# Many-head attention: tokens on the partitions in the product, one batch projected ahead of the other, values awaited later, norms by batch

## The reference

```
x = x + L2_attn(layernorm(x))    # 16 query heads of 16 wide, 4 key/value heads, causal
x = x + L2_ffn(layernorm(x))     # x @ (sum of 8 factor matrices) / sqrt(8) + bias
x = x + L3_xattn(layernorm(x))   # 16 heads of 128 wide over 2048 context tokens
x = x + L3_attn(layernorm(x))    # differential attention, see below
x = x + L3_ffn(layernorm(x))
# L2_attn
q, k, v = x @ Wq, x @ Wk, x @ Wv
out = softmax(causal(q k^T / 4)) v ;  return out @ Wo
# L3_attn: 32 half heads of 8 wide, values 16 wide, a pair of half heads per head
probs = softmax(causal(q k^T / sqrt(8)))
attn = (probs[0] - lam * probs[1]) v ; attn = attn * rms(attn) * g * 0.8 ; return attn @ Wo + bo
```

## Time and profile before

| | |
|---|---|
| timed runs (3) | median 1151.47 us, 1148.25 to 1151.93 |
| profiled execution | 1146.93 us |
| its span | 1145.0 us |
| PE busy | 1044.0 us, 91% of the span |
| DVE, ACT, POOL busy | 61%, 44%, 20% |
| mean granted clock of PE | 0.974 |

### The profile page before, as it was taken

One profiled execution on the slowest core, in us unless ns is written; L12 is line 12 of the kernel. 1 busy time (PEld: TensorE's weight loads), 2 busy tenths in 40 slices (PEclk: granted clock), 3 DMA queues, 4 the chain that ended last, 5 costly groups with the idle time before them and its releaser, 6 DMA issues.

```text
span 1145.0 us, 23185 instructions
## 1 busy us (share of the span) xinstructions
PE 1044.0 (91%) x9488; PEld 847.0 (74%) x9488; DVE 700.8 (61%) x1333; ACT 505.3 (44%) x871; POOL 233.2 (20%) x356
## 2 busy tenths in 40 slices
PE   6988999979999879999988799989999999999785
PEld 3755788856667546767765688889999999999664
DVE  3655343267776368888644666766656466667366
ACT  3232131226767248888764423332332222332374
POOL 5601058102132000000011311210001133332120
PEclk9999999989999889999999999999999999999897
DMA  9621447536652417000131211121111121100000
GB/s 389 266 77 76 148 168 224 174 92 173 177 161 80 162 49 244 2 2 2 41 145 37 92 37 38 36 103 47 38 39 55 46 76 56 56 20 10 0 2 10
DMA packets 39332, 104.57 MB, mean 91 GB/s; under 512 B 4160, under 2 KB 12736, under 8 KB 37568
## 3 DMA queue, kind: packets, MB, share of 16 engines
q1 hardware_dynamic: 35328, 91.55, 24.2%
q0 software_dynamic: 2752, 9.44, 2.4%
q10 hardware_dynamic: 1152, 2.16, 0.5%
HBM read 87.93 MB, written 15.20 MB: 90 GB/s over the span
## 4 chain that ended last, share of the span: by engine, by line
PE 74%; DVE 12%; ACT 5%; POOL 4%; issue 3%; DMA 2%; DVEq 0%; SPq 0%; ACTq 0%; POOLq 0%
PE ps L2184 9%; PE ps L390 8%; PE ps L2139 7%; PE ps L1372 5%; PE ps L1723 5%; PE ps L383 4%; PE ps L2029 4%; PE ps L446 3%; PE ps L1714 3%; PE ps L1520 3%; PE ps L2043 2%; PE ps L1058 2%; PE ps L1531 2%; PE ps L1050 2%; DVE st L1649 2%
## 5 line engine op out<-in xcount | busy, mean ns | idle before, releaser
L2184 PE MATMUL ps<-vv,prob 128*128 128x129 f32 x1024 | 128.7, 275 | 0.0
L2184 PEld LDWEIGHTS ps<-vv,prob 128*128 128x128 f32 x1024 | 122.5, 192 | 0.0
L2307 DVE TENSOR_REDUCE probT<-ps 128x128 f32<-128x1024 f32 x64 | 82.6, 1290 | 28.8 <-PE ps L2139 20.8
L1649 DVE TENSOR_REDUCE st<-ps 128x1 f32<-128x512 f32 x128 | 83.5, 687 | 25.3 <-PE ps L1520 19.1
L2074 ACT ACTIVATE kt<-ps,w 128x512 f32<-128x512 f32 x32 | 22.0, 688 | 141.8 <-PE ps L2051 141.8
L390 PE MATMUL ps<-xT,big 128*128 128x256 f32 x352 | 79.6, 380 | 0.8 <-ACT xT L673 0.7
L2319 DVE TENSOR_TENSOR prob<-ps,probT 128x1024 f32<-128x1024 f32 x64 | 79.6, 1286 | 1.1
L2280 ACT ACTIVATE prob<-prob 128x1024 f32<-128x1024 f32 x64 | 70.7, 1107 | 19.6 <-DVE prob L2319 19.6
L1596 ACT ACTIVATE prob<-ps 128x1024 f32<-128x1024 f32 x64 | 65.7, 1028 | 27.8 <-PE ps L1531 26.1
L152 POOL TENSOR_SCALAR small<-small 128x4 f32<-128x4 f32 (+1 forms) x44 | 12.0, 272 | 322.2 <-DVE small L2081 175.3
L390 PEld LDWEIGHTS ps<-xT,big 128*128 128x128 f32 x352 | 66.5, 190 | 10.7 <-ACT xT L673 0.9
(11 more groups left out here) (457 smaller groups left out, 2214.4 us busy)
## 6 DMA issues: line engine op xcount, KB each, us to landing
big<-ctxT_in SPq DMA_DIRECT2D x36, 512.0 KB, 4.1
big<-blocks_in SPq DMA_DIRECT2D x22, 768.0 KB, 4.4
key_parts<-w POOLq DMA_DIRECT2D x16, 384.0 KB, 4.7
kt<-key_parts SPq DMA_DIRECT2D x32, 192.0 KB, 3.3
vv<-ctx_in SPq DMA_DIRECT2D x2, 2176.0 KB, 23.9
vv<-early_values SPq DMA_DIRECT2D x4, 1088.0 KB, 12.9
kt<-ctxT_in SPq DMA_DIRECT2D x2, 2048.0 KB, 11.4
kt<-key_parts SPq DMA_DIRECT2D x32, 128.0 KB, 3.1
```

Source lines behind the costliest of these rows:

```text
L1649: dve.tensor_reduce(self.mx[:, u % 2, n:n + 1], k.ps[:, n % 2, :], AX.X, ALU.max).then_inc(s("reduced"), 1)
L2184: last = pe.matmul(k.ps[:, 7, 0:DH + 1], self.prob(u)[:, ch * P:ch * P + P], v, start=(ch == 0), stop=(ch == MC))
L2307: dve.tensor_reduce(self.largest[:, h * P:(h + 1) * P], bank.rearrange("p (c t) -> p t c", t=P), AX.X, ALU.max).then_inc(s("c3_max"), 1)
```

## The change

- `Heads.product`: `probT` (128x128) becomes the stationary operand and v with its ones (17 columns) the moving one. The result has tokens on the partitions, 17 columns per head, in bank 6 or 7 by turns. `ot`, `back` and the zeroing of bank 6 go; `finish` reads the product's bank; the reciprocals have two buffers.
- `Heads.tensor` takes two callbacks: `values_ready` waits ahead of product 0 for the values and the ones, which the layers awaited ahead of everything; `turn_first` turns batch 0 of `att` ahead of the last product.
- Both layers: v is projected into bank 6 instead of 2. Batch 0 is projected behind the last product, then batch 1 is turned, copied and projected. In L2 this replaces one turn, one copy and one projection of both batches; L3 did it by batch already, behind all units.
- Norms 7 to 10: each batch's transposes go to a bank of their own, each with a semaphore count, and ACT copies each batch; one count of `xT` at the end.
- Norm 10: the statistics of batch 0 are taken ahead of the wait for the last projection of batch 1.
- `Differential.vector`: the scaling of g is moved ahead of the wait for lam's exponentials.

```diff
+    BY_BATCH = {7: (7, 0), 8: (7, 2), 9: (7, 3), 10: (7, 3)}
...
+    def tensor_batches(k, pe, n):
+        for b, bank in enumerate(Norm.BY_BATCH[n]):
+            pe.wait_ge(k.s("norm_xn"), 2 * n + b + 1)
+            turn_batch(k, pe, k.xn, b, bank, 0).then_inc(k.s("norm_turned"), 1)
...
+    def scalar_batches(k, act, n):
+        for b, bank in enumerate(Norm.BY_BATCH[n]):
+            act.wait_ge(k.s("norm_turned"), Norm.turned_batches(n, b))
+            last = act.copy(k.xT[:, b].rearrange("p c t -> p (c t)"), k.ps[:, bank, 0:D])
+        last.then_inc(k.s("xT"), 1)
...
+def copy_att(k, act, b, count):
+    act.wait_ge(k.s("att_turned"), count)
+    act.copy(k.attT[:, b].rearrange("p c t -> p (c t)"), k.ps[:, b, 0:D]).then_inc(k.s("attT"), 1)
...
+    def output(self, i):
+        return self.k.ps[:, 6 + i % 2, 0:8 * 17].rearrange("p (h n) -> p h n", n=17)
...
-            if i >= 1:
-                pe.wait_ge(*self.at("ot", i))
+            if i >= 2:
+                pe.wait_ge(*self.at("out", i - 1))
             for h in range(8):
-                g = h % 4 * 32
-                last = pe.matmul(k.ps[g:g + 17, 6, h // 4 * P:h // 4 * P + P], self.v[:, b, kv(h)], k.probT[:, h * P:(h + 1) * P], start=True, stop=True)
+                last = pe.matmul(self.output(i)[:, h], k.probT[:, h * P:(h + 1) * P], self.v[:, b, kv(h)], start=True, stop=True)
             last.then_inc(self.s("product"), 1)
-        def back(i):
...
             if i + 2 < n:
                 scores(i + 2)
+            if i == 0:
+                values_ready()
+            if i == n - 1:
+                turn_first()
             product(i)
-            if i >= 1:
-                back(i - 1)
-        back(n - 1)
...
-        def ot(i):
...
-            dve.wait_ge(*self.at("back", i + 1))
+            dve.wait_ge(*self.at("product", i + 1))
...
-        o.step(dve.memset(k.ps[:, 6, 0:256], 0.0))
...
         pe.wait_ge(s("g2_sb"), 2)
-        pe.wait_ge(s("heads_ones"), 2)
-        self.heads.tensor(pe)
-        pe.wait_ge(s("att"), 2)
-        turn(k, pe, k.att, 7).then_inc(s("att_turned"), 1)
+        def values_ready():
+            pe.wait_ge(s("g2_sb"), 3)
+            pe.wait_ge(s("heads_ones"), 1)
+        def turn_first():
+            pe.wait_ge(s("heads_out"), 2)
+            turn_batch(k, pe, k.att, 0, 0, 0).then_inc(s("att_turned"), 1)
+        self.heads.tensor(pe, values_ready, turn_first)
         pe.wait_ge(s("attT"), 2)
-        for b in range(B):
-            last = project(k, pe, k.ps[:, 3, b * D:(b + 1) * D], k.attT, b, w("Wo", DC), D)
+        project(k, pe, k.ps[:, 3, 0:D], k.attT, 0, w("Wo", DC), D)
+        pe.wait_ge(s("heads_out"), 4)
+        turn_batch(k, pe, k.att, 1, 1, 0).then_inc(s("att_turned"), 1)
+        pe.wait_ge(s("attT"), 3)
+        project(k, pe, k.ps[:, 3, D:2 * D], k.attT, 1, w("Wo", DC), D).then_inc(s("out_projection"), 1)
...
-        act.copy(flat(self.heads.kk), k.bank(1))
+        act.copy(flat(self.heads.kk), k.bank(1)).then_inc(s("g2_sb"), 1)
...
+        dve.wait_ge(s("w_added"), 1)
+        Norm.stats(k, dve, o, 0)
         dve.wait_ge(s("w_wo"), 2)
-        dve.wait_ge(s("w_added"), 1)
         o.step(dve.tensor_tensor(k.x[:, 1], k.x[:, 1], k.ps[:, 6, 0:D], ALU.add))
+        Norm.stats(k, dve, o, 1)
...
         pe.wait_ge(s("e3_sb"), 3)
-        pe.wait_ge(s("e3_lam"), 2)
-        pe.wait_ge(s("heads_ones"), 4)
-        self.heads.tensor(pe)
+        def values_ready():
+            pe.wait_ge(s("e3_lam"), 2)
+            pe.wait_ge(s("heads_ones"), 2)
+        def turn_first():
+            pe.wait_ge(s("att"), 2)
+            turn_batch(k, pe, k.att, 0, 0, 0).then_inc(s("att_turned"), 1)
+        self.heads.tensor(pe, values_ready, turn_first)
...
         self.heads.scalar(act)
+        copy_att(k, act, 0, 4)
         self.table(act, ACT.Sqrt, 504)
-        self.copy_att(act, 0)
...
```

More of the change, by code:

```diff
@@ L216, in tensor, with turned_batches @@
         last.then_inc(k.s("norm_turned"), 1)
+    BY_BATCH = {7: (7, 0), 8: (7, 2), 9: (7, 3), 10: (7, 3)}
+    @staticmethod
+    def turned_batches(n, b):
+        return turned_norms(n - 1) + sum(i in Norm.BY_BATCH for i in range(n)) + b + 1
+    @staticmethod
+    def tensor_batches(k, pe, n):
+        for b, bank in enumerate(Norm.BY_BATCH[n]):
+            pe.wait_ge(k.s("norm_xn"), 2 * n + b + 1)
+            turn_batch(k, pe, k.xn, b, bank, 0).then_inc(k.s("norm_turned"), 1)
+    @staticmethod
+    def scalar_batches(k, act, n):
[3 more added lines that the diff above has]
+        last.then_inc(k.s("xT"), 1)
     @staticmethod
@@ L1288, in scalar @@
         act.wait_ge(s("g2_proj"), 2)
-        act.copy(flat(self.heads.kk), k.bank(1))
+        act.copy(flat(self.heads.kk), k.bank(1)).then_inc(s("g2_sb"), 1)
         act.wait_ge(s("g2_proj"), 3)
-        act.copy(self.heads.v[:, :, :, 0:16], k.bank(2, 128).rearrange("p (b h n) -> p b h n", b=B, h=4)).then_inc(s("g2_sb"), 1)
+        act.copy(self.heads.v[:, :, :, 0:16], k.bank(6, 128).rearrange("p (b h n) -> p b h n", b=B, h=4)).then_inc(s("g2_sb"), 1)
         self.heads.scalar(act)
-        act.wait_ge(s("att_turned"), 2)
-        act.copy(flat(k.attT), k.bank(7)).then_inc(s("attT"), 1)
+        copy_att(k, act, 0, 2)
+        copy_att(k, act, 1, 3)
     def vector(self, dve, o):
@@ L2499, in vector @@
         dve.sem_inc(s("e3_lam"), 1)
+        o.step(dve.tensor_scalar(self.g, w("g"), 0.8, None, ALU.mult))
         dve.wait_ge(s("e3_sb"), 1)
@@ L2765, in _ @@
             wide.value(pe, 5, 3)
-            Norm.tensor(k, pe, 7)
+            Norm.tensor_batches(k, pe, 7)
             pe.wait_ge(s("w_v_sb"), 4)
@@ L2769, in _ @@
             wide.value(pe, 2, 1)
-            Norm.tensor(k, pe, 8)
+            Norm.tensor_batches(k, pe, 8)
             pe.wait_ge(s("xT"), turned_norms(8))
@@ L2776, in _ @@
             wide.value(pe, 3, 2)
-            Norm.tensor(k, pe, 9)
+            Norm.tensor_batches(k, pe, 9)
             wide.tensor(pe)
-            Norm.tensor(k, pe, 10)
+            Norm.tensor_batches(k, pe, 10)
             differential.tensor(pe)
@@ L2827, in _ @@
             wide.copy_value(act, 5, 3)
-            Norm.scalar(k, act, 7)
+            Norm.scalar_batches(k, act, 7)
             Norm.table(k, act, ACT.Exp, 3)
@@ L2835, in _ @@
                 wide.copy_value(act, *((2, 1) if n == 8 else (3, 2)))
-                Norm.scalar(k, act, n)
+                Norm.scalar_batches(k, act, n)
             Norm.table(k, act, ACT.Exp, 5)
@@ L2841, in _ @@
                 Norm.root(k, act, 10, b)
-            Norm.scalar(k, act, 10)
+            Norm.scalar_batches(k, act, 10)
             differential.scalar(act)
@@ L2920, in _ @@
             wide.vector(dve, o, eight)
-            Norm.vector(k, dve, o, 10)
+            Norm.scaled(k, dve, o, 10)
             differential.vector(dve, o)
```

48 lines of the change are left out of this document (16 added, 32 removed).

## The result

The changed kernel takes 1159.56 us (median of 12 runs), the kernel before 1150.18 beside it: ratio 1.0087, 95% interval 1.0066 to 1.0108. One execution of before (5146 us) and two of the changed kernel (1787 and 2105 us) were far slower, why is not known, and the ratio leaves them out. A second series gave 1.0096 (1.0072 to 1.0119). That is 10 us slower, where +3.0 was forecast; it is where the rival "clock falls earlier" stood (1159.8). The profiled execution of the changed kernel took 1158.35 us (span 1156.4, mean granted clock 0.964 against 0.974).

A forecast was written before the change was run, and what follows sets the result against it. PE was taken as the bound, with 74% of the chain of waits. L2 +1.0, norms 7 to 9 -0.35, norm 10 -0.65, start of L3 -2.1, its loop +5.5, end -0.4: +3.0 us, 1154.5; range 1147 to 1160.

The forecast's parts named there:

- clock falls earlier: Rival, chance 0.20: clock falls one product sooner in each many-head layer, transposes and product double; about +8 us, 1159.8.
- The product: Probabilities times values in each unit: 16 records at 0.111 us, 1.78 us against 0.56; bounds 0.97 and 1.94.
- Loop of L3: Second many-head layer, 8 units: a PE-bound unit takes 4.38 us, before 3.33; the loop gains +5.5 us of length.
- L2: First many-head layer: loop net +3.2 us; end at 608.4 against 607.45 with the clock taken as fallen; together +1.0.
- The prediction's own line for full clock: End of the first many-head layer, should the clock stay full: 606.3, that is -1.1 us.
- Norms and start of L3: Norm 10: smaller copy, earlier statistics, -0.65 us; second many-head layer's first scores released by ACT's k copy, -2.1.
- the lower bound of 1.6: Start of the second many-head layer: gain of 1.6 us if the value bias on DVE (0.43) came into the way.
- norms 7 to 9: Norms copied by batch: -0.2 us for norm 8, -0.2 for norm 9, +0.05 for norm 7; together -0.35.
- End of L3: End of the second many-head layer: batch 0's projection runs earlier, while DVE combines batch 1; -0.4 us.
- The added waits: PE's waits ahead of each layer's first and last product: awaited work done before, no term in the sum.
- Clock holds: Rival, chance 0.20: 2.4 GHz at the second many-head layer's first projection and the first's end; -2.4 us, 1149.1.
- Loads overlap: Rival, chance 0.15: 0.061 us a record, product 0.97 us in both many-head layers; -3.9 us, 1147.6.

The follow-up runs named there:

- e8: Changed kernel with each head's 17 columns of values moving three times in a row (51 columns a record): 1149.20 us, ratio to before 0.9999.
- e3: Changed kernel with three unused bf16 128x512 matmuls ahead of the product in the last two units of each layer: 1150.19 us, ratio to before 1.0010.
- e6: Changed kernel with six unused f32 128x128 transposes ahead of the product in the last two units of each layer: 1147.90 us, ratio to before 1.0001.
- e7: Changed kernel with three unused f32 matmuls, 17 columns moving, ahead of each layer's last two products: 1158.02 us, ratio to before 1.0079.
- e4: Changed kernel with turned probabilities and values in bf16 for the product: 1138.01 us, ratio to before 0.9917.
- e1: Changed kernel with the old product put back, with its ACT copy, transposes back and memset: 1146.08 us, ratio to before 0.9987.
- e2: Kernel before with the new product alone, without transposes back and their ACT copy: 1162.82 us, ratio to before 1.0128.
- e5: Kernel before with three unused bf16 128x512 matmuls ahead of the product in the last two units of each layer: 1150.17 us, ratio 1.0006.

## Why the prediction was wrong

**The product** (forecast 1.78, bounds 0.97 and 1.94): 1.70. A row of the same shape elsewhere in the trace gave the price to 5%. In fact the loads stand 0.111 apart, exactly as there; I counted 16 such steps where there are 15, and the transposes' first load follows 0.03 behind the last one. That three times the stream costs nothing beside the load is shown by e8.

**Loop of L3** (+5.5): with the clock held, 36.4 - 31.2 = +5.2 (e3, e6, e8), right. In the changed kernel +7.1 and +7.6: product 7 at 1.2 GHz (its loads take 3.49 instead of 1.86, 1.63 more) is most of the rest.

**L2** (+1.0, and 0.35 more in this stretch, as that gain lies ahead of it): +3.6 against the profiled execution that I used, +5.2 in the means. This is the step that failed, and its sentence is "I take the clock as fallen at that point, as now": it left products 2 and 3 of L2, and product 7 of L3, at full clock. I put the fall behind product 3 for both kernels, because the trace of before had it there. In the changed kernel it comes ahead of product 3 (3.49) and in a second execution at the start of product 2; and in before's second execution it isn't there at all, so the cold projection that I counted on both sides was not a constant. With the clock held L2 is 21.8, +0.2 to the mean of before. The prediction's own line for full clock, 606.3, comes to 21.6 (606.3 less the first maximum at 585.04, that one expected 0.35 earlier); so what is not the clock was priced to 0.2 us.

**Norms and start of L3** (-0.65 and -2.1, together -2.75): the stretch shrank by 4.2 in the first pair of traces. 1.3 of that is the projection at another mix of clock levels (5.41 against 6.71), the rest 2.9. From the sum to the projection it is 3.07 instead of 3.81: -0.74. Scores released by ACT's k copy, as said, and 2.1 earlier than in the first trace of before. But here too one execution was taken for the kernel: the scaling of g on DVE (line 2506), ahead of the memset that held the scores, took 1.03 us in that trace and 0.24 in before's second:

```profile
1086.89 1.03 DVE L2506 TENSOR_SCALAR small<-w 128x16 f32<-128x16 f32 x1
```

```profile
1086.98 0.24 DVE L2506 TENSOR_SCALAR small<-w 128x16 f32<-128x16 f32 x1
```

Against the second trace the scores gain 1.5, just under the lower bound of 1.6. The norms 7 to 9 (-0.35) were not measured alone. From L2's sum to the sum ahead of norm 10, with norms 8 and 9 between, it is 467.6 and 466.4 us before and 467.5 and 467.9 after, so no gain shows there.

**End of L3** (-0.4): batch 0's sum stands 2.33 behind the last reciprocal, 2.73 before; right in that pair, though before's second trace has 2.34 as well.

**The added waits** cost nothing that a trace shows.

**The rivals.** "Clock falls earlier" had the mechanism, its place in both layers and nearly its time (+8, against 10), at a chance of 0.20. That 1159.8 lies so close to 1159.56 is partly luck: it stands on the median of three early runs of before, 1.3 us above the later one, and it prices the fall at 2.65 in each layer, where the changed kernel stands 5.0 above the held clock in L2 and 2.1 in L3. What I held against it, clock 1.00 in 596 to 600 with PE busy for 2.17 of 4 us, was a window in which each record moved 128 columns or more. In the changed kernel PE is busier there and the records of the product move 17; I weighed the busy time alone, and in e7 PE was busy throughout and the clock fell all the same. "Clock holds" happened in the variants e6 and e8 at L3's projection (start 9.5 instead of 11.1), not in the changed kernel. "Loads overlap" is refuted by the product's 1.70.

What stays open: against the means of before, the four stretches sum to +0.4 for e8 (measured -0.1), +9.2 for the changed kernel (+10), -9.4 for e4 (-9.5), but to -5.9 for e1, where the ratio says -1.5 (-3.7 to +0.8), and to +17.0 for e2 (+14.7, traced in its slowest execution). Two traces of one kernel differ by 1.6 in L2 and 2.0 in the start with nothing changed, so such sums close to some us and no better; whether the other edits without the new product win 3 us or nothing is not shown. Nor is it shown what decides at which product an execution loses its clock.

## What to carry to other kernels

Exchanging the sides of a matmul exchanges the load and the stream: with 128 f32 columns stationary and 17 moving a record costs 0.106 us, and PE looks busy while little moves. Where a price is read from a row at full clock, ask also what the new instruction does to the clock: here the same work with 51 columns moving instead of 17 was 10 us faster. A feature of one profiled execution, such as a cold stretch or one slow DVE instruction, should be seen in a second trace before it is put on both sides of a sum.

## What the runs showed of the hardware

- Three copies of a 17-column product cost no more than one (1.71 against 1.70 us for 16 records), and kept 2.4 GHz where one copy lost it.
- Some 0.65 us of transposes or of 512-column bf16 matmuls ahead of the last two products of a layer kept the granted clock at 1.00 past them; as much of 17-column matmuls did not (0.52 and 0.50).
- A bf16 128x128 weight load of the product followed the last one in 0.024 us, an f32 one in 0.106 on average.
- One kernel's executions differ by some 12 us (1141.54 to 1153.97 in 30 runs of before), and traces show clock falls at 87 us and at L2's end that come and go.
- One DVE instruction, 128x16 elements, took 1.03, 0.24, 0.80 and 0.17 us in four traces in which it stood in the same place (before twice, e2, e5).
